# One slot's norm before the other's, and single products moved between others

## The reference

```python
# L1_xattn: x is normed, attends to itself (a1), is normed again, attends to the context (a2)
x = _ln(xx, ln1_g, ln1_b)
x = x + _mha(x, x, ..., causal=True)       # a1
x = _ln(x, ln2_g, ln2_b)
return x + _mha(x, ee, ..., causal=False)  # a2
# inside _mha
xn = _ln(x, lnx_g, lnx_b); yn = _ln(y, lny_g, lny_b)
...
x_out = x + o @ li1_w + li1_b
h = gelu(_ln(x_out, ln3_g, ln3_b) @ li2_w + li2_b)
return x_out + h @ li3_w + li3_b

# L1_ffn: scores above the diagonal are 0, not minus infinity, before the softmax
att = where(tril, q @ k.T, 0.0) / sqrt(d)
out = softmax(att) @ v          # so values of later tokens count too, each with exp(0 - max)
...                             # each token goes to one of 8 experts, with a capacity
return (x2 - mean) / sqrt(var + 1e-05) * gamma + beta

# L2_ffn: a router picks 2 of 4 experts for each token
router_logits = gelu(x @ rW1 + rb1) @ rW2 + rb2
out = sum over e of (gelu(xi @ We1[e] + be1[e]) @ We2[e] + be2[e]) * combine_w[e]
```

## Time and profile before

| | us |
|---|---|
| three executions, median (lowest, highest) | 1772.88 (1769.68, 1773.03) |
| profiled execution | 1774.03 |
| its span, first to last instruction | 1772.3 |
| TensorE busy in it | 1523.8 (86%) |
| VectorE busy | 870.2 (49%) |
| ScalarE busy | 744.5 (42%) |
| GpSimd busy | 148.9 (8%) |

### The profile page before, as it was taken

The page is one execution under the profiler, slowest core; times in us unless marked ns, Lnnn a source line. Parts: engine busy times, 40 slices in busy tenths (PEclk is TensorE's granted clock), DMA queues, the critical chain, the costliest instruction groups (busy, mean ns, idle before and its releaser), DMA issues.

```text
span 1772.3 us, 21984 instructions
## 1 busy us (share of the span) xinstructions
PE 1523.8 (86%) x8796; PEld 686.8 (39%) x8814; DVE 870.2 (49%) x1674; ACT 744.5 (42%) x1313; POOL 148.9 (8%) x209
## 2 busy tenths in 40 slices
PE   5748999889899989988479999898999889888296
PEld 2223333342344436623133333423444347433284
DVE  4464776443556453334645884524664541446212
ACT  2553556323445325243544555243454153252043
POOL 0000111100012000000000112000021000011331
PEclk9968999999899989998779999999899989999598
DMA  4000000000000100000000000000000100030241
GB/s 196 1 1 0 1 1 1 0 1 1 0 1 1 48 1 0 1 1 2 1 1 1 1 1 1 0 1 1 1 1 6 43 0 1 1 83 1 81 137 61
DMA packets 18105, 30.27 MB, mean 17 GB/s; under 512 B 4640, under 2 KB 12640, under 8 KB 17104
## 3 DMA queue, kind: packets, MB, share of 16 engines
q1 hardware_dynamic: 16752, 26.23, 4.6%
q0 software_dynamic: 1248, 2.59, 0.4%
HBM read 23.62 MB, written 5.19 MB: 16 GB/s over the span
## 4 chain that ended last, share of the span: by engine, by line
PE 78%; DVE 9%; ACT 8%; issue 2%; DMA 1%; POOL 1%; SPq 0%; POOLq 0%; DVEq 0%; ACTq 0%
PE ps L837 7%; PE ps L944 5%; PE ps L711 4%; PE ps L883 4%; PE ps L651 3%; PE ps L1399 3%; PE ps L1411 3%; PE ps L1075 3%; PE ps L750 3%; PE ps L1083 2%; PE ps L995 2%; PE ps L896 2%; PE ps L975 2%; PE ps L688 2%; PE ps L684 2%
## 5 line engine op out<-in xcount | busy, mean ns | idle before, releaser
L2102 DVE TENSOR_REDUCE peak<-ps 128x1 f32<-128x512 f32 x256 | 163.1, 682 | 97.4 <-PE ps L837 97.4
L1714 ACT ACTIVATE big<-ps 128x512 f32<-128x512 f32 x256 | 138.5, 596 | 114.1 <-PE ps L875 113.9
L837 PE MATMUL ps<-pp,qT 32*128 32x512 f32 x512 | 148.7, 668 | 1.4 <-ACT pp L1837 1.4
L866 PE MATMUL ps<-qT,pp 32*128 32x512 f32 x512 | 148.2, 653 | 0.0
L1737 ACT ACTIVATE big<-ps 128x512 f32<-128x512 f32 (+3 forms) x256 | 101.1, 436 | 101.4 <-PE ps L975 100.4
L2147 DVE TENSOR_REDUCE crest<-ps 128x2 f32<-128x512 f32 (+3 forms) x128 | 105.2, 824 | 66.4 <-PE ps L950 66.3
L975 PE MATMUL ps<-qT,pp 32*128 32x128 f32 (+3 forms) x512 | 123.1, 479 | 0.0
L1653 ACT ACTIVATE big<-ps 77x1024 f32<-77x1024 f32 x96 | 93.2, 1017 | 65.8 <-PE ps L711 65.8
L2043 DVE TENSOR_REDUCE small<-ps 128x8 f32<-128x616 f32 x96 | 76.8, 800 | 80.7 <-PE ps L684 46.4
L944 PE MATMUL ps<-pp,qT 32*128 32x384 f32 (+3 forms) x512 | 110.5, 502 | 5.0 <-DVE crest L2147 3.0
L1633 ACT ACTIVATE sq<-ps 128x512 f32<-128x512 f32 x48 | 28.7, 597 | 192.7 <-PE ps L651 192.7
(11 more groups left out here) (492 smaller groups left out, 2686.0 us busy)
## 6 DMA issues: line engine op xcount, KB each, us to landing
big<-in_w SPq DMA_DIRECT2D x23, 256.0 KB, 3.3
pt<-in_l2w SPq DMA_DIRECT2D x2, 2048.0 KB, 7.6
w_l<-in_l SPq DMA_DIRECT2D x1, 3086.0 KB, 18.2
pp<-in_w SPq DMA_DIRECT2D x1, 2048.0 KB, 9.9
big<-by_expert SPq DMA_DIRECT2D x23, 66.0 KB, 2.0
by_expert<-cst SPq DMA_DIRECT2D x1, 1472.0 KB, 16.6
cst<-in_const SPq DMA_DIRECT2D x1, 1427.5 KB, 7.1
w_l<-in_l SPq DMA_DIRECT2D x1, 1218.0 KB, 9.2
```

The costliest lines, as they stand in the source:

```text
L837: pe.matmul(rbank(x), qT[at, u, k, 128 * i:128 * i + 128], keyT(u, k)[at, :], start=True, stop=True, tile_position=(32 * c, 0)).then_inc(* ...
L866: pe.matmul(a1_bank(y), keyT(u, k)[at, 128 * j:128 * j + 128], qT[at, u, k, :], start=True, stop=False, tile_position=(32 * c, 0))
L1714: A(prob(m)[:, TURN_OF[g], :], a1_bank(tplace(m, g)), ACT.Exp).then_inc(*SCALAR.did("a1", "exp", m, g))
L2102: v.tensor_reduce(peak[:, p // 4 % 2, i, c:c + 1], rbank(ring(p, c)), AX.X, ALU.max)\
```

## The change

In VectorE's program, `norm` gets a third argument that is called for a slot right after that slot's multiplication; `affine` handles one slot. In the seven places with an affine, VectorE now ends slot 0 (multiplication, affines, and behind "l1g" the residual too) and then slot 1. The number of instructions and their sizes are the same.

On TensorE, the first projections use the banks in the order 0, 6, 7, 1, and the third and fourth projection wait for slot 1's reciprocal root and slot 1's multiplication, which read those banks. The suffix products are made one at a time, each behind a pair of row scores of steps 1 to 4. Slot 0's router logits stay in front of the experts; slot 1's go one block of tokens at a time behind each of the first four expert products. The bias of the experts is one product of 512 columns for each slot, made for both slots before the sums with the identity, which add to it.

The core of the diff:

```diff
-            return PSB[(0, 1, 6, 7)[n % 4]]
+            return PSB[(0, 6, 7, 1)[n % 4]]
...
+                def suffix(u, j):
+                    if j == 3:
+                        pe.wait_ge(*VECTOR["l1f v", u])
+                    mm = pe.matmul(PSB[5 - 5 * u][:, 0:128 * (j + 1)], x2[:, u, 128 * j:128 * j + 128],
+                                   K["later"][:, 384 - 128 * j:512], start=j == 3, stop=j == 0)
...
                         if c % 2:
                             diagonals(p, c // 2)
+                            if p:
+                                suffix((p - 1) // 2, 3 - 2 * ((p - 1) % 2) - c // 2)
...
-                for u in U:
-                    suffix(u)
...
+                        elif n == 2:
+                            pe.wait_ge(*SCALAR["l1b", "rs", 1])
+                        elif n == 3:
+                            pe.wait_ge(*VECTOR["l1b", "n", 1])
...
+                pe.wait_ge(*SCALAR["l2f r", 0])
+                for i in range(4):
+                    routed(0, i)
+                pe.wait_ge(*SCALAR["l2f r", 1])
...
                         pe.matmul(scb(c), l2e[:, 512 * e + 128 * c:512 * e + 128 * c + 128], xn[:, u, :], start=True,
                                   stop=True).then_inc(*TENSOR.did("l2f up", n, c))
+                        if n == 0:
+                            routed(1, c)
...
                 for u in U:
                     pe.wait_ge(*VECTOR["l2f cwT", u])
+                    pe.matmul(aux(u), part[0:E2, 0, 0:128], cwT(u, E2), start=True, stop=False, skip_group_check=True)
+                for u in U:
                     pe.wait_ge(*VECTOR["l2f out", 2 * E2 - 2 + u])
                     for i in range(4):
-                        pe.matmul(aux(u)[:, 128 * i:128 * i + 128], x2[:, u, 128 * i:128 * i + 128], ident, start=True,
-                                  stop=False)
-                        mm = pe.matmul(aux(u)[:, 128 * i:128 * i + 128], part[0:E2, 0, 0:128],
-                                       cwT(u, E2)[:, 128 * i:128 * i + 128], start=False, stop=True)
+                        mm = pe.matmul(aux(u)[:, 128 * i:128 * i + 128], x2[:, u, 128 * i:128 * i + 128], ident, start=False,
+                                       stop=True, skip_group_check=True)
...
-            def norm(tag, dst):
+            def norm(tag, dst, then=lambda u: None):
                 for u in U:
                     v.wait_ge(*SCALAR[tag, "rs", u])
                     v.tensor_tensor(dst(u), lin(u), rs[:, u, :], ALU.mult).then_inc(*VECTOR.did(tag, "n", u))
+                    then(u)
...
-                norm("l1b", lambda u: xn[:, u, :])
-                affine("a1 y", lambda u: x2[:, u, :], lambda u: xn[:, u, :], w["a1_lny_g"], w["a1_lny_b"])
-                affine("a1 in", lambda u: xn[:, u, :], lambda u: xn[:, u, :], w["a1_lnx_g"], w["a1_lnx_b"])
+                def twofold(u):
+                    affine("a1 y", u, x2, xn, w["a1_lny_g"], w["a1_lny_b"])
+                    affine("a1 in", u, xn, xn, w["a1_lnx_g"], w["a1_lnx_b"])
+                norm("l1b", lambda u: xn[:, u, :], twofold)
...
+                def added(u):
+                    affine("l1g aff", u, xn, xn, w["gamma"], w["beta"])
                     v.wait_ge(*VECTOR["l1g aff", u])
                     residual("l1f res", u, xn[:, u, :], 5)
+                norm("l1g", lambda u: xn[:, u, :], added)
```

More of the change, by code:

```diff
@@ L976, in colscore @@
                               stop=True, tile_position=(32 * c, 0)).then_inc(*TENSOR.did("l1f", "T", n, g))
[L978 to L983, removed]
+                def suffix(u, j):
[3 more added lines that the diff above has]
+                                   K["later"][:, 384 - 128 * j:512], start=j == 3, stop=j == 0)
+                    if j == 0:
+                        mm.then_inc(*TENSOR.did("l1f", "suffix", u))
                 def values(n):
@@ L1384, in _, with routed @@
                     mm.then_inc(*TENSOR.did("l2f r", u))
[L1385 to L1391, removed]
+                def routed(u, i):
+                    for c in range(2):
+                        mm = pe.matmul(aux(u)[:, 16 * i:16 * i + E2], hid[u][:, c, 128 * i:128 * i + 128],
+                                       w["rW2"][:, E2 * c:E2 * c + E2], start=c == 0, stop=c == 1)
+                    if i == 3:
+                        mm.then_inc(*TENSOR.did("l2f logits", u))
+                pe.wait_ge(*SCALAR["l2f r", 0])
+                for i in range(4):
+                    routed(0, i)
+                pe.wait_ge(*SCALAR["l2f r", 1])
                 pe.wait_ge(l2_loaded, 16)
@@ L1995, in norm, with affine @@
                     v.tensor_tensor(dst(u), lin(u), rs[:, u, :], ALU.mult).then_inc(*VECTOR.did(tag, "n", u))
-            def affine(name, dst, src, g, b):
-                for u in U:
-                    v.wait_ge(*VECTOR.last())
-                    v.tensor_scalar(dst(u), src(u), g, b, ALU.mult, ALU.add).then_inc(*VECTOR.did(name, u))
+                    then(u)
+            def affine(name, u, dst, src, g, b):
+                v.wait_ge(*VECTOR.last())
+                v.tensor_scalar(dst[:, u, :], src[:, u, :], g, b, ALU.mult, ALU.add).then_inc(*VECTOR.did(name, u))
             def residual(tag, u, y, g, bias=None):
@@ L2393, in _ @@
                                     W["l1"]["a2_lny_b"], ALU.mult, ALU.add).then_inc(*VECTOR.did())
-                norm("l1o", lambda u: x1[:, u, :])
-                affine("l1 x1", lambda u: x1[:, u, :], lambda u: x1[:, u, :], w["ln1_g"], w["ln1_b"])
-                norm("l1b", lambda u: xn[:, u, :])
-                affine("a1 y", lambda u: x2[:, u, :], lambda u: xn[:, u, :], w["a1_lny_g"], w["a1_lny_b"])
-                affine("a1 in", lambda u: xn[:, u, :], lambda u: xn[:, u, :], w["a1_lnx_g"], w["a1_lnx_b"])
+                norm("l1o", lambda u: x1[:, u, :], lambda u: affine("l1 x1", u, x1, x1, w["ln1_g"], w["ln1_b"]))
+                def twofold(u):
+                    affine("a1 y", u, x2, xn, w["a1_lny_g"], w["a1_lny_b"])
+                    affine("a1 in", u, xn, xn, w["a1_lnx_g"], w["a1_lnx_b"])
+                norm("l1b", lambda u: xn[:, u, :], twofold)
                 def joined(u):
@@ L2405, in _ @@
                 attend(joined)
-                norm("a1n3", lambda u: xn[:, u, :])
-                affine("a1m in", lambda u: xn[:, u, :], lambda u: xn[:, u, :], w["a1_ln3_g"], w["a1_ln3_b"])
+                norm("a1n3", lambda u: xn[:, u, :], lambda u: affine("a1m in", u, xn, xn, w["a1_ln3_g"], w["a1_ln3_b"]))
                 for u in U:
@@ L2412, in _ @@
                 context_kv("a2", None, 32)
-                norm("l1c", lambda u: x1[:, u, :])
-                affine("l1c x1", lambda u: x1[:, u, :], lambda u: x1[:, u, :], w["ln2_g"], w["ln2_b"])
-                norm("l1d", lambda u: xn[:, u, :])
-                affine("a2 in", lambda u: xn[:, u, :], lambda u: xn[:, u, :], w["a2_lnx_g"], w["a2_lnx_b"])
+                norm("l1c", lambda u: x1[:, u, :], lambda u: affine("l1c x1", u, x1, x1, w["ln2_g"], w["ln2_b"]))
+                norm("l1d", lambda u: xn[:, u, :], lambda u: affine("a2 in", u, xn, xn, w["a2_lnx_g"], w["a2_lnx_b"]))
                 for u in U:
@@ L2429, in _ @@
                         .then_inc(*VECTOR.did("a2 x2", u))
-                norm("a2n3", lambda u: xn[:, u, :])
-                affine("a2m in", lambda u: xn[:, u, :], lambda u: xn[:, u, :], w["a2_ln3_g"], w["a2_ln3_b"])
+                norm("a2n3", lambda u: xn[:, u, :], lambda u: affine("a2m in", u, xn, xn, w["a2_ln3_g"], w["a2_ln3_b"]))
                 for u in U:
@@ L2524, in _ @@
                 mixed(1)
-                norm("l1g", lambda u: xn[:, u, :])
-                affine("l1g aff", lambda u: xn[:, u, :], lambda u: xn[:, u, :], w["gamma"], w["beta"])
-                for u in U:
+                def added(u):
+                    affine("l1g aff", u, xn, xn, w["gamma"], w["beta"])
                     v.wait_ge(*VECTOR["l1g aff", u])
                     residual("l1f res", u, xn[:, u, :], 5)
+                norm("l1g", lambda u: xn[:, u, :], added)
                 w = W["l2"]
```

## The result

| | before | changed |
|---|---|---|
| median (lowest to highest), us | 1771.37 (1769.68 to 1773.03) | 1721.41 (1716.33 to 1725.82) |
| profiled execution, its span, us | 1774.03, 1772.3 | 1725.82, 1724.0 |
| mean granted clock in it | 0.921 | 0.934 |

The ratio is 0.9717, with a 95% interval of 0.9683 to 0.9751: 50 us less, where 42 were forecast. In a later series of five executions the changed kernel took 1715.29 (ratio 0.9675, 0.9658 to 0.9692). Ratios are of mean times, so they can differ a little from those of the medians; two executions further down, one of them of the kernel before, took 7 and 16% longer at a mean clock of 0.80 and 0.71 and are left out.

What follows compares the result with a forecast made beforehand. TensorE, at 78% of the span, was taken to bound the kernel through its waits for VectorE and the low clock behind them. 1774.0 less 22.7 (order), 19.3 (clock) and 1.15 gave 1731 us; range for 8 in 10, 1714 to 1756.

Steps and rivals of the forecast that it cites:

- The bound, and the double price of a wait: TensorE's standing still for VectorE costs the time: the wait itself, and often a low clock behind it.
- Plain stages by order: Two MLPs and the second attention's queries, twice per run: product 1.24 us sooner each, 7.4 us; full clock adds 6.0.
- Norm before a norm: Four places where another norm follows directly: 4.5 us by order, 2.6 us by a clock staying full.
- First projections: In front of the first attention: query product 1.9 us sooner, 3.8 us in two turns; clock 2.4, half counted.
- "l1g": Residual done slot by slot behind "l1g": 1.3 us twice, 2.6 us; nothing counted for the clock.
- Suffix: Suffix products among the row scores: 1.2 us by order, 6.8 by clock, two thirds of 10.2.
- Logits: Slot 1's router logits among the first expert products: zero by order, 1.5 us by clock, half of 3.1.
- Expert bias: Sums' block from 6.9 us to 5.0 to 5.3, identity products about 0.41 each: 1.6 us per turn, 3.2.
- rival (b): All stretches hold full clock, 29.5 us from the clock: 1721 us; chance 0.16.
- Rival (a): The order's 22.7 us come through and the clock's gain does not: 1750 us; chance 0.22.
- (c): Slot 1's affine sets the end at norm places, only 0.3 to 0.5 us each: 1762 us; chance 0.06.
- (d): Slower: suffix products among narrow row scores keep the clock low into the long loop; 1780 us; chance 0.03.

Runs made afterwards that it cites:

- the first three experiments: Kernel before with VectorE's part alone, 1741.82 us; with TensorE's three parts alone, 1751.5; in its old order with unused products ahead of six waits, 1768.03.

## Why the forecast held, and which terms were off

- **The bound, and the double price of a wait.** Right: VectorE's work is the same, its share of the chain too, and the gain is TensorE's waits and its clock.
- **Plain stages by order, 7.4.** Right: where the clock was full before and after (the second MLP, both turns) the stage took 22.32 and takes 21.09, 1.23. With the clock's 6.0 the term was 13.4, and 11.45 was measured. The missing 2 lie in turn 1 in the second attention behind the queries, where the clock is low for 13.65 us (399 to 413) and was for 6.83. To count all six places as full was wrong in one: the queries of turn 2 took 8.80 us for 7.11, within what the forecast named as a sign of being wrong. A later low stretch that came out shorter, 10.24 us for 13.65, hides this in the sum.
- **Norm before a norm, 4.5 and 2.6 of clock.** 6.31. At full clock before and after 0.95 (0.8 reckoned), where the clock came back 2.56. Behind the same wait of 1.89 us it held in two places of four and fell in two (turn 1 at "l1d", 8.52 to 7.56 us).
- **First projections, 3.8 and 2.4.** 8.13. The query product starts 1.82 us sooner in both turns; the clock held behind the wait of 2.47 us in turn 1 and fell behind 2.52 in turn 2, the half that was counted. The surplus is turn 2's: the low stretch behind the wait and one further on took 3.41 us each where they had taken 6.83, some 2 us of time together, which no step foresaw.
- **"l1g", 2.6 and no clock.** 3.05, and the clock stayed low, as said, though in turn 2 for half as long.
- **Suffix, 1.2 and 6.8.** The stretch gave 4.93 and 5.04 us in the two turns: it is at full clock without a wait, so all came back, more than the two thirds taken. What failed is the step that ends the account there: 4.9 of the 10.0 us were lost again among the experts of the same layer, so 5.11 came through. Alone the suffix part gained the kernel perhaps 2.5. The Trainium skill, "TensorE: Matmul & The Clock Gate", section "A second HAM failure mode: psum-queue depth-cycling", says that frequent small idles between groups of products can make the clock swing. The trace agrees in the layers that fell: the experts' products wait 0.35, 0.72 and 0.39 us, and the clock is low behind; in as many layers with the same waits it was not. What the forecast drew from that section, that one wait cut into two gives no clock back, did not hold in front of the plain stages: full in five of six places, where three were before.
- **Logits, 0 and 1.5.** From the first logit to the first product of the second layer 12.12 us became 10.44, 1.7 in each turn: all that was open came, where half was taken.
- **Expert bias, 3.2.** The step most off, 11.5 instead. The block takes 3.89 for 6.91 us, 3.0 per turn: I let the identity products keep 0.41 each, the price that they had only in turns with the thin ones. And from the block's end to the next norm 5.35 us instead of 8.12, 2.8 per turn: a low clock behind the thin products stood only as a danger of the new order, not as a cost of the old one. Behind thin products in a row, in the experiment with the bias in blocks, it was low in one turn of two. That the thin products bring it is likely by this and not shown by itself.
- **The sum.** 42.0 forecast, 48.2 in the profile. Above: bias 8.3, logits 1.9, projections 1.9, "l1g" 0.5; below: suffix 2.9, plain stages 2.0, norms before a norm 0.8, places without a term 0.6. The profiled execution is the longest of the four, 4.4 us over their median, where 1.15 was reckoned, and this is the rest of the way from 1731 to 1721. That the time lies on rival (b)'s 1721 is chance of the sum: stretches at the norms before a norm, at the queries, at "l1g" and among the experts did not hold, and the bias made up for it. Rival (a) fell with the first three experiments, and (c) by the 1.23 us that a plain stage gave at full clock. (d) did not come, since the row scores ran at full clock in both turns; the whole block placed early did something like it, a low clock that reached into the long loop.

## What to carry to other kernels

Read the rows behind a wait of TensorE as well as the wait: a product that takes twice its time there is part of the price, and it can be had back by unused products in the wait even where the order can't be changed. Count a clock that is spared at the end of the kernel, not of the stretch: a small wait further on may take it. Count it only where the others wait for TensorE: a higher mean clock is no gain in itself. And put products of one kind next to each other before making them wider.

## What the hardware showed that was not expected

- Products of 128 columns with 128 and with 4 rows took 0.42 us each in turns, 0.25 each when eight of a kind stood together, at full clock in both cases. Which part of the alternation costs it was not tried.
- The experts' stretch with the same waits fell to half the clock in five of ten layers. That alone makes 5 us of difference between executions, and the changed kernel spreads over 10 us from 1710 to 1720 in one series; with this wait and four others filled 1704 to 1709.
- The clock fell where TensorE had hardly waited: with the block of suffix products early, after 10.66 us of work in 10.85, among products on 32 rows. With nine waits filled it fell once where TensorE did not wait at all: for 6.83 us near the end of L1_ffn's long loop, among products on 32 rows.
